# Routers of three layers: weights stand still, 512 turned tokens move, logits turned back

## The chip, the cores and the metric

One core of one Trainium2 chip. The metric is the device time of one execution of the kernel in microseconds (us). Engines: PE (TensorE, matrix multiplication), with PEld for its weight loads; DVE (VectorE); ACT (ScalarE); POOL (GpSimd); SP (SyncE, which here only issues transfers).

## What is computed

A stack of four layers on 32 x 256 = 8192 tokens of width 128, all in float32. Each layer is a mixing part and a part with experts, both added to the residual. Four times a router scores the tokens against the experts. For layers 0, 1 and 2, cut to what matters:

```
x = x + _L0_attn_ref(_layernorm(x), ...)
x = x + _L0_ffn_ref(_layernorm(x), ...)      # scores = softmax(h @ gate_w.T), 16 experts
x = x + _L1_attn_ref(_layernorm(x), ...)
x = x + _L1_ffn_ref(_layernorm(x), ...)      # logits = h @ gate_w + gate_b, 8 experts, top 2
x = x + _L2_attn_ref(_layernorm(x), ...)
x = x + _L2_ffn_ref(_layernorm(x), ...)      # logits = h @ router_W.T + router_b, 6 experts, top 2
```

Here `h` is the normalised x. Layer 3's router has 4 + 8 = 12 outputs and works on a normalisation with gain and offset.

## The kernel before

x stays on chip as 64 tiles of 128 tokens (tokens on the partitions). The kernel is a sequence of blocks; in most of them each engine runs its own loop over NU = 16 steps of UT = 4 tiles (U = 512 tokens), and the engines wait for each other by semaphores. A block ends when all engines have ended their loops; then the next begins.

`route` (line 849) is such a block. It is called for layer 0 as "d" (line 942, 16 outputs, no bias), for layer 1 as "m1" (line 1901, 8 outputs), for layer 2 as "m2" (line 2525, 6 outputs) and for layer 3 as "m3" (line 2752, 12 outputs, with `affine`). Its parts, for step n:

- DVE, `normed`: waits until PE has turned the tiles of step n - 3, then normalises four tiles (line 394, in `norm_tiles`) into one of S = 3 buffers nrm.
- PE, `turn`: transposes the four tiles (line 403, in `turn_tiles`) into a PSUM bank ps_t, so that the width is on the partitions and 512 tokens lie side by side.
- ACT, `keep`: copies the bank to hT (line 921), and for layers 1 and 2 first to h_all as well (line 920), which later loops use.
- PE, `project` (line 908): for each of the four tiles one matmul whose stationary operand is the tile of hT (128 x 128) and whose moving operand is the router's weights (16, 8 or 6 columns). The result has tokens on the partitions, in a bank ps_l. The first operand after the output in a `matmul` call is the stationary one.
- DVE, `keep`: waits for the logits and copies them to `logits` (line 892), or adds the bias on the way (line 894).

`staggered(eng, units, slots, *stages)` (line 107) sets the order on one engine: in step s it issues each stage in the order given, for unit s - lag. DVE runs (0, normed), (3, keep); PE runs (2, project), (0, turn); ACT runs (0, keep). An engine executes its instructions strictly in that order, and a wait holds up all that comes behind it. `sig.now(n, 1)` waits for unit n, `sig.ago(n, 1, S)` for unit n - S, `sig.last(n, 1)` for unit n - 1.
Of the kernel before, what the change touches and what calls it, by code (L numbers as in the profile page):

```python
# [12 lines left out]
ACT = mybir.ActivationFunctionType  # L13
# [4 lines left out]
ds = bass.ds  # L18

P = 128  # L20
# [3 lines left out]
UT = 4  # L24
U = UT * P
NU = NT // UT
# [80 lines left out]
def staggered(eng, units, slots, *stages):  # L107

    deep = max(lag for lag, _ in stages)
    rounds = (units - deep) // slots

    def step(i, s):
        for lag, work in stages:
            n = s - lag
            if i is not None:
                work(i * slots + n, n % slots, i + n // slots)
            elif 0 <= n < units:  # L120
                work(n, n % slots, n // slots)

    for s in range(deep):
        step(None, s)
    with eng.Fori(0, rounds) as i:  # L125
        for v in range(slots):
            step(i, deep + v)
    for s in range(deep + rounds * slots, units + deep):
        step(None, s)
# [43 lines left out]
def build(nc, x_in, pack_in, maskb_in, w0_in, w1_in, w3_in, out, ktab, ychan, q_stack, k_stack, ones_rows, v_ones,  # L173
          m_parts, xs1, xs3, ys):
    ctx = ExitStack()
    with ctx:
# [5 lines left out]
        def sig(name, per):  # L182
            return Signal(pool, name, per)

        def sb(name, shape, dt=F32, stack=ctx):
            return stack.enter_context(nc.sbuf_tensor(name, shape, dt))

        def bank(name, stack, n=1):
            return stack.enter_context(nc.psum_tensor(name, [P, n, 512], F32))
# [15 lines left out]
        ident = c("ident")  # L205
# [62 lines left out]
        routes = {}  # L268
        for t in ("d", "m1", "m2", "m3"):
            routes[t] = (Front(t, 1), sig(t + "_logits", 1), sig(t + "_logits_kept", 1), sig(t + "_affine", 2),  # L270
                         sig(t + "_src_kept", 1))
        g_n, g_p, g_mm, g_x = sig("g_normed", 4), sig("g_onehot", 4), sig("g_gathered", 4), sig("g_stored", 4)
        x_w, x_gu, x_ge, x_h, x_o, x_s = ([sig(f"x_weights{j}", 16) for j in range(2)], sig("x_gate_up", 8), sig("x_gelu", 8),
                                         sig("x_hidden", 8), sig("x_down", 4), sig("x_kept", 4))
# [123 lines left out]
        def turn_tiles(pe, done, ps, nrm, n, *waits):  # L398

            for w in waits:  # L400
                pe.wait_ge(*w)
            for t in range(n):
                ins = pe.transpose(ps[:, t * P:(t + 1) * P], nrm[:, t, :], ident)
            ins.then_inc(done.sem, 1)
# [133 lines left out]
        with ExitStack() as st_u:  # L538
            u_all = sb("u_all", [P, TPB, NB, INNER], stack=st_u)
            with ExitStack() as st:  # L540
                S = 4
                nrm = sb("a_nrm", [P, UT, P], stack=st)
                hT = [sb(f"a_hT{j}", [P, U], stack=st) for j in range(S)]
# [182 lines left out]
        with ExitStack() as st:  # L726
            S = 3
            nrm = sb("c_nrm", [P, UT, P], stack=st)
            hT = [sb(f"c_hT{j}", [P, U], stack=st) for j in range(S)]
# [119 lines left out]
        def route(tag, src, weights, bias, n_out, logits, h_all=None, affine=None, fetch=None):  # L849

            fr, lg, kept, aff, put = routes[tag]
            S = 3
            with ExitStack() as st:
                nrm = [sb(f"{tag}_nrm{j}", [P, UT, P], stack=st) for j in range(S)]
                hT = [sb(f"{tag}_hT{j}", [P, U], stack=st) for j in range(S)]
                ps_t = bank(f"{tag}_ps_t", st, S)
                ps_l = bank(f"{tag}_ps_l", st, S)  # L860
                with pool.loop_block(NU) as block:
                    if fetch is not None:
                        @block.sync
                        def _(sp):
                            w, w_in = fetch
                            for e in range(w.shape[1]):
                                n_filled[0] += 16
                                sp.dma_start(w[:, e, :], w_in[e]).then_inc(filled, 16)
                            sp.wait_ge(filled, n_filled[0])

                    @block.vector
                    def _(dve):
                        def normed(n, j, r):
                            free = fr.tps.ago(n, 1, S)
                            if affine is None:
                                norm_tiles(dve, fr.nrm, nrm[j], src, n * UT, UT, rstd, free)
                                return
                            dve.wait_ge(*put.ago(n, 1, S))
                            norm_tiles(dve, aff, nrm[j], src, n * UT, UT, rstd, free)
                            dve.wait_ge(*aff.now(n, 1))  # L880
                            dve.tensor_tensor(nrm[j][:, :, :], nrm[j][:, :, :],
                                              affine[0].unsqueeze(1).to_broadcast([P, UT, D]), ALU.mult).then_inc(aff.sem, 1)
                            dve.wait_ge(*aff.now(n, 2))
                            dve.tensor_tensor(nrm[j][:, :, :], nrm[j][:, :, :],
                                              affine[1].unsqueeze(1).to_broadcast([P, UT, D]), ALU.add
                                              ).then_inc(fr.nrm.sem, 1)

                        def keep(n, j, r):
                            dve.wait_ge(*lg.now(n, 1))
                            to, got = logits[:, ds(n * UT, UT), :], ps_l[:, j, 0:UT * n_out].rearrange("p (t e) -> p t e", t=UT)  # L890
                            if bias is None:
                                ins = dve.tensor_copy(to, got)
                            else:
                                ins = dve.tensor_tensor(to, got, bias.unsqueeze(1).to_broadcast([P, UT, n_out]), ALU.add)
                            ins.then_inc(kept.sem, 1)

                        staggered(dve, NU, S, (0, normed), (3, keep))

                    @block.tensor
                    def _(pe):  # L900
                        def turn(n, j, r):
                            turn_tiles(pe, fr.tps, ps_t[:, j, :], nrm[j], UT, fr.nrm.now(n, 1), fr.hT.ago(n, 1, S))

                        def project(n, j, r):
                            pe.wait_ge(*fr.hT.now(n, 1))
                            pe.wait_ge(*kept.ago(n, 1, S))
                            for t in range(UT):
                                ins = pe.matmul(ps_l[:, j, t * n_out:(t + 1) * n_out], hT[j][:, t * P:(t + 1) * P], weights,
                                                start=True, stop=True)
                            ins.then_inc(lg.sem, 1)  # L910

                        staggered(pe, NU, S, (2, project), (0, turn))

                    @block.scalar
                    def _(act):
                        def keep(n, j, r):
                            act.wait_ge(*fr.tps.now(n, 1))
                            act.wait_ge(*lg.ago(n, 1, S))
                            if h_all is not None:
                                act.activation(h_all[:, ds(n * U, U)], ps_t[:, j, :], ACT.Copy)  # L920
                            act.activation(hT[j][:, :], ps_t[:, j, :], ACT.Copy).then_inc(fr.hT.sem, 1)
                            if affine is not None:
                                act.activation(src[:, ds(n * UT, UT), :], nrm[j][:, :, :], ACT.Copy).then_inc(put.sem, 1)

                        staggered(act, NU, S, (0, keep))

        def softmax_rows(dve, lg, out_e, m, s, n):

# [10 lines left out]
        with ExitStack() as st_d:  # L939
# [72 lines left out]
            with ExitStack() as st_x:  # L1012
# [3 lines left out]
                with ExitStack() as st:  # L1016
                    S = 4
# [126 lines left out]
                with ExitStack() as st:  # L1144
                    S = 3
# [3 lines left out]
                    hT, hotT, eo, ge, hs = ([sb(f"f_{n}{j}", [P] + shape, stack=st) for j in range(S)] for n, shape in (  # L1149
                        ("hT", [SEQ]), ("hotT", [4, SEQ]), ("eo", [4, D]), ("ge", [2, SEQ]), ("hs", [2, SEQ])))  # L1150
# [123 lines left out]
        with ExitStack() as st:  # L1274
            VW = D + 4
            S = 6
            nrm, hT, egate, gate, qk, low, v1, am = (
                [sb(f"l_{n}{j}", [P] + shape, stack=st) for j in range(S)] for n, shape in (
                    ("nrm", [TPB, P]), ("hT", [SEQ]), ("egate", [SEQ]), ("gate", [SEQ]), ("qk", [2, SEQ]), ("low", [2, SEQ]),
                    ("v", [TPB, VW]), ("am", [P + SEQ])))  # L1280
# [614 lines left out]
        with ExitStack() as st1:  # L1895
# [3 lines left out]
            lg = sb("lg1", [P, NT, E1], stack=st1)  # L1899
            w = sb("w1", [P, E1, wide(F1)], stack=st1)  # L1900
            route("m1", x_res, c("gate1"), c("gate1b"), E1, lg, h_all, fetch=(w, w1_in))
            with ExitStack() as st:
                t1 = sb("m1_t", [P, NT], stack=st)
                with nc.Block() as block:
# [16 lines left out]
                    def _(act):  # L1921
# [3 lines left out]
                           normed=(h_all, x_res))  # L1925
# [595 lines left out]
        with ExitStack() as st2:  # L2521
            h_all = sb("h_all2", [P, NT * P], stack=st2)
            comb = sb("comb2", [P, NT, E2 + 1], stack=st2)
            lg = sb("lg2", [P, NT, E2], stack=st2)
# [28 lines left out]
            with ExitStack() as st:  # L2553
                S = 3
                hT = [sb(f"m_hT{j}", [P, U], stack=st) for j in range(S)]
# [79 lines left out]
        with ExitStack() as st:  # L2635
            S = 3
            nrm = sb("s_nrm", [P, UT, P], stack=st)
            hT = [sb(f"s_hT{j}", [P, 2, SEQ + 1], stack=st) for j in range(S)]
# [101 lines left out]
        with ExitStack() as st3:  # L2740
# [5 lines left out]
            with ExitStack() as st:  # L2746
# [4 lines left out]
                lg = sb("lg3", [P, NT, G3 + E3], stack=stl)  # L2751
# [40 lines left out]
            with ExitStack() as st:  # L2792
                S = 6
# [179 lines left out]
```

## Time and profile before

| | us |
|---|---|
| median of 3 runs | 3575.7 (3569.54 to 3576.92) |
| profiled execution, time | 3574.73 |
| its span | 3572.9 |
| PE busy in the span | 2609.7 (73%) |
| DVE busy | 2245.5 (63%) |
| ACT busy | 1580.3 (44%) |
| POOL busy | 634.1 (18%) |
| mean granted clock | 0.859 |

The span is the profiled part of one execution; the time has a little around it. PE's busy time is not PE at its peak, since passes overlap and also run at half clock. The granted clock of PE is 1.00 at 2.4 GHz and 0.50 at 1.2 GHz.

How the views are read. The page's slices cut the span into 40 equal parts. A window row gives the length of a stretch, the busy time of each engine with its number of instructions, the granted clock (PEclk), the share of the DMA engines that was busy, and what they moved. A timeline row gives start, duration (of a merged run: from first start to last end), engine, line, operation, tiles and form, count, and in brackets how long the engine had been idle before and what ended that. "128*128 128x16 f32" means 128 rows and 128 columns of weights, and a moving operand of 16 columns.

### The profile page before, as it was taken

To read this page: it belongs to the slowest core of one execution; us is meant where nothing else is said; L and a number is where in the kernel's file an instruction comes from. 1 tells how busy PE (TensorE), PEld (TensorE's weight loads), DVE (VectorE), ACT (ScalarE), POOL (GpSimd) and SP (SyncE) were. 2 spreads that over 40 slices of the span, in tenths; PEclk is the share of its full clock that TensorE was granted. 3 is DMA by queue.
4 is the path that set the end of the run, shared out by engine and by line. 5 is a ranking of instruction groups with operands and counts; after the bars stand their busy time and mean duration, and the time that the engine had idled before them with its cause. 6 is when DMAs were issued, how large, how long until landed. Compare 5 with 4: busy or idle time off the path is not lost. (4 is left out here: it accounts for less than half of the span.)

```text
span 3572.9 us, 72294 instructions
## 1 busy us (share of the span) xinstructions
PE 2609.7 (73%) x20194; PEld 1892.7 (53%) x20194; DVE 2245.5 (63%) x4945; ACT 1580.3 (44%) x3615; POOL 634.1 (18%) x873
## 2 busy tenths in 40 slices
PE   3546749999987576998339999966565999973280
PEld 1333444459877433998226777756333555552270
DVE  5924966248777422776846666645885777765267
ACT  2503613334364233775235666632253667751253
POOL 0000100000000265554301111100120111102553
PEclk7878959999998687999679999968797999985585
DMA  3096100100091011222494565400097555510123
GB/s 94 7 258 176 53 0 18 35 18 0 0 156 54 20 46 43 70 69 89 152 276 62 71 73 71 57 1 1 0 293 109 69 68 75 71 43 19 53 77 100
DMA packets 335935, 263.34 MB, mean 74 GB/s; under 512 B 23132, under 2 KB 317452, under 8 KB 335308
## 3 DMA queue, kind: packets, MB, share of 16 engines
q1 hardware_dynamic: 314200, 227.03, 31.5%
q0 software_dynamic: 12928, 26.70, 2.2%
q10 hardware_dynamic: 8704, 8.39, 0.8%
q8 instruction: 46, 0.75, 0.1%
q14 instruction: 57, 0.47, 0.0%
HBM read 145.60 MB, written 114.86 MB: 73 GB/s over the span
## 5 line engine op out<-in xcount | busy, mean ns | idle before, releaser
L2444 ACT ACTIVATE h_pt<-h_ps 128x384 f32<-128x384 f32 (+1 forms) x1024 | 543.6, 545 | 306.2 <-PE h_ps L2353 151.8
L2197 DVE TENSOR_REDUCE h_nm<-h_ps 128x4 f32<-128x1024 f32 (+1 forms) x448 | 539.7, 1220 | 163.4 <-PE h_ps L2324 64.0
L1606 POOL DMA_INDIRECT sorted_rows<-e_row,e_pos x192 | 185.1, 964 | 443.4 <-DVE e_row L1585 239.6
L2372 PE MATMUL h_ps_o<-h_pt,h_vp 128*32 128x256 f32 (+1 forms) x4096 | 246.8, 358 | 1.3 <-ACT h_pt L2444 1.3
L1796 POOL DMA_INDIRECT results<-e_y,e_ykey x208 | 211.0, 1015 | 193.6 <-DVE e_y L1785 176.7
L1843 ACT ACTIVATE e_hid<-e_ps_h,e_wt 128x128 f32<-128x128 f32 x688 | 204.3, 369 | 27.7 <-PE e_ps_h L1817 19.0
L2358 PE MATMUL h_ps<-h_sq,h_sk 128*128 128x256 bf16 x1024 | 193.6, 275 | 23.9 <-DMA h_sq<-m_parts 13.6
L1817 PE MATMUL e_ps_h<-e_hT,e_wt 128*128 128x128 f32 x1376 | 201.9, 288 | 6.3 <-issue 2.6
L1825 PE MATMUL e_ps_o<-e_wt,e_hid 128*128 128x128 f32 x1376 | 198.0, 283 | 11.2 <-ACT e_hid L1843 10.4
L1753 DVE TENSOR_SCALAR e_wt<-w 128x1156 f32 (+1 forms) x208 | 140.0, 673 | 98.5 <-DVE e_y L1785 69.8
L1817 PEld LDWEIGHTS e_ps_h<-e_hT,e_wt 128*128 128x128 f32 x1376 | 179.7, 201 | 14.2 <-issue 10.4
L1825 PEld LDWEIGHTS e_ps_o<-e_wt,e_hid 128*128 128x128 f32 x1376 | 178.2, 199 | 15.9 <-ACT e_hid L1843 13.5
L2295 PE MATMUL h_ps<-h_sk,h_sq 128*128 128x256 bf16 x1024 | 157.1, 277 | 39.7 <-DVE h_identb L2179 34.5
L2243 POOL TENSOR_TENSOR h_mpart<-h_nm,h_zero 128x32 bf16<-128x32 f32 x64 | 15.3, 240 | 892.5 <-DVE h_nm L2197 892.5
L2372 PEld LDWEIGHTS h_ps_o<-h_pt,h_vp 128*32 128x32 f32 x4096 | 106.8, 109 | 92.5 <-issue 36.7
L1810 PE MATMUL e_ps_t<-pack,e_xt 128*128 128x128 f32 x208 | 59.2, 286 | 124.9 <-DMA e_xt<-sorted_rows 124.3
L2350 PE MATMUL h_ps<-h_sq,h_sk 128*128 128x256 bf16 x512 | 140.6, 275 | 6.6 <-ACT h_pt L2444 2.8
L2353 PE MATMUL h_ps<-h_mskb 128*128 128x256 bf16 x512 | 139.6, 273 | 0.0
L1140 DVE TENSOR_TENSOR x_hid<-x_gelu,x_ps_u 128x512 f32<-128x512 f32 x64 | 43.4, 688 | 141.8 <-ACT x_gelu L1125 141.8
L2307 PE MATMUL h_ps<-h_sk,h_sq 128*128 128x256 bf16 x512 | 98.2, 274 | 45.7 <-DVE h_identb L2179 44.3
L2358 PEld LDWEIGHTS h_ps<-h_sq,h_sk 128*128 128x128 bf16 x1024 | 81.5, 98 | 93.1 <-ACT h_pt L2444 80.6
L2295 PEld LDWEIGHTS h_ps<-h_sk,h_sq 128*128 128x128 bf16 x1024 | 98.4, 99 | 58.7 <-DVE h_identb L2179 34.7
(435 smaller groups left out, 6170.8 us busy)
## 6 DMA issues: line engine op xcount, KB each, us to landing
h_sq<-q_stack SPq DMA_DIRECT2D x64, 384.0 KB
h_sk<-k_stack SPq DMA_DIRECT2D x64, 384.0 KB
sorted_rows<-pad SPq DMA_DIRECT2D x26, 520.0 KB, 11.7
e_xt<-sorted_rows SPq DMA_DIRECT2D x104, 130.0 KB, 2.2
e_got<-results SPq DMA_DIRECT2D x24, 512.0 KB, 5.9
q_stack<-p_parts SPq DMA_DIRECT2D x32, 384.0 KB, 3.1
k_stack<-p_parts SPq DMA_DIRECT2D x32, 384.0 KB, 3.8
v_ones<-p_v SPq DMA_DIRECT2D x32, 288.0 KB, 2.7
```

The costliest lines, as they stand in the source:

```text
L1606: gp.indirect_dma_start(xs[:, :], bass.IndirectOffsetOnAxis(ap=pos[:, n % choices, tile:tile + 1], axis=0), row[n % ROWS][:, :], None).the ...
L1753: dve.tensor_scalar(wt[j % 4][:, :], w[:, :, :].rearrange("p e w -> p (e w)")[:, ds(at, wc)], 1.0, None, ALU.mult).then_inc(e_w.sem, 1)
L1796: gp.indirect_dma_start(ys[:, :], bass.IndirectOffsetOnAxis(ap=key[m // 4][:, m % 4:m % 4 + 1], axis=0), y[m][:, :], None).then_inc(return ...
L1817: pe.matmul(ps_h[:, k, 0:P], wt[j % 4][:, f * P:(f + 1) * P], hT[j % 4][:, :], start=True, stop=True).then_inc(e_h.sem, 1)
L1825: ins = pe.matmul(o, hid_t[m][:, f, :], wt[m][:, f_dim + f * D:f_dim + (f + 1) * D], start=(f == 0), stop=(f == nf - 1))
L1843: act.activation(hid_t[j % 4][:, f, :], ps_h[:, (j * nf + f) % 4, 0:P], func, bias=wt[j % 4][:, o_b1 + f:o_b1 + f + 1]).then_inc(e_a.sem, 1)
L2197: dve.tensor_reduce(to, got, AX, ALU.max, negate=True).then_inc(s["mx"].sem, 1)
L2295: ins = pe.matmul(ps_1[:, h % 4, q * SEQ:(q + 1) * SEQ], sq[u][:, h, q * P:(q + 1) * P], sk[u][:, h, :], start=True, stop=True)
L2350: pe.matmul(o[:, 0:SEQ], sk[u][:, hd, 0:P], sq[u][:, hd, :], start=True, stop=False, skip_group_check=True)
L2358: ins = pe.matmul(o[:, t * SEQ:(t + 1) * SEQ], sk[u][:, hd, t * P:(t + 1) * P], sq[u][:, hd, :], start=True, stop=True)
L2372: ins = pe.matmul(ps_o[32 * j:32 * (j + 1), q0:], vp[u % 2][:, t, head(HG * g + j), :], pt[g % 2][:, j, t * SEQ:(t + 1) * SEQ - q0], start ...
L2444: act.activation(pt[g % 2][:, j, :], ps_2[:, h % 2, 0:SW], ACT.Exp, scale=scale).then_inc(s["ex"].sem, 1)
```

## The change

In `route`, where there is no `affine` (d, m1, m2), the logits are computed the other way round. The router's weights are the stationary operand and the 512 tokens of hT move, in one matmul; the logits come out with experts on the partitions (16, 8 or 6 of them) and 512 tokens side by side, in a bank ps_f of 3. ACT copies them to lT (`keep_flat`). PE turns them back with four matmuls whose stationary operand is a piece of lT (16, 8 or 6 rows, 128 columns) and whose moving operand is the corner of the unit matrix (16, 8 or 6 columns), into a single bank ps_l. DVE's `keep` comes a step later (lag 4) and reads from that bank. PE runs (3, turn_back), (2, project_flat), (0, turn); ACT runs (0, keep), (2, keep_flat). Layer 3's router is unchanged.

```diff
--- before.py
+++ after.py
@@ -268,7 +268,7 @@
         routes = {}
         for t in ("d", "m1", "m2", "m3"):
             routes[t] = (Front(t, 1), sig(t + "_logits", 1), sig(t + "_logits_kept", 1), sig(t + "_affine", 2),
-                         sig(t + "_src_kept", 1))
+                         sig(t + "_src_kept", 1), sig(t + "_logits_flat", 1), sig(t + "_flat_kept", 1))
         g_n, g_p, g_mm, g_x = sig("g_normed", 4), sig("g_onehot", 4), sig("g_gathered", 4), sig("g_stored", 4)
         x_w, x_gu, x_ge, x_h, x_o, x_s = ([sig(f"x_weights{j}", 16) for j in range(2)], sig("x_gate_up", 8), sig("x_gelu", 8),
                                          sig("x_hidden", 8), sig("x_down", 4), sig("x_kept", 4))
@@ -851,13 +851,17 @@
 
 
 
-            fr, lg, kept, aff, put = routes[tag]
+            fr, lg, kept, aff, put, flat, flat_kept = routes[tag]
+            by_expert = affine is None
             S = 3
             with ExitStack() as st:
                 nrm = [sb(f"{tag}_nrm{j}", [P, UT, P], stack=st) for j in range(S)]
                 hT = [sb(f"{tag}_hT{j}", [P, U], stack=st) for j in range(S)]
                 ps_t = bank(f"{tag}_ps_t", st, S)
-                ps_l = bank(f"{tag}_ps_l", st, S)
+                if by_expert:
+                    lT = [sb(f"{tag}_lT{j}", [n_out, U], stack=st) for j in range(S)]
+                    ps_f = bank(f"{tag}_ps_f", st, S)
+                ps_l = bank(f"{tag}_ps_l", st, 1 if by_expert else S)
                 with pool.loop_block(NU) as block:
                     if fetch is not None:
                         @block.sync
@@ -887,19 +891,33 @@
 
                         def keep(n, j, r):
                             dve.wait_ge(*lg.now(n, 1))
-                            to, got = logits[:, ds(n * UT, UT), :], ps_l[:, j, 0:UT * n_out].rearrange("p (t e) -> p t e", t=UT)
+                            to = logits[:, ds(n * UT, UT), :]
+                            got = ps_l[:, 0 if by_expert else j, 0:UT * n_out].rearrange("p (t e) -> p t e", t=UT)
                             if bias is None:
                                 ins = dve.tensor_copy(to, got)
                             else:
                                 ins = dve.tensor_tensor(to, got, bias.unsqueeze(1).to_broadcast([P, UT, n_out]), ALU.add)
                             ins.then_inc(kept.sem, 1)
 
-                        staggered(dve, NU, S, (0, normed), (3, keep))
+                        staggered(dve, NU, S, (0, normed), (4 if by_expert else 3, keep))
 
                     @block.tensor
                     def _(pe):
                         def turn(n, j, r):
                             turn_tiles(pe, fr.tps, ps_t[:, j, :], nrm[j], UT, fr.nrm.now(n, 1), fr.hT.ago(n, 1, S))
+
+                        def project_flat(n, j, r):
+                            pe.wait_ge(*fr.hT.now(n, 1))
+                            pe.wait_ge(*flat_kept.ago(n, 1, S))
+                            pe.matmul(ps_f[0:n_out, j, :], weights, hT[j][:, :], start=True, stop=True).then_inc(flat.sem, 1)
+
+                        def turn_back(n, j, r):
+                            pe.wait_ge(*flat_kept.now(n, 1))
+                            pe.wait_ge(*kept.last(n, 1))
+                            for t in range(UT):
+                                ins = pe.matmul(ps_l[:, 0, t * n_out:(t + 1) * n_out], lT[j][:, t * P:(t + 1) * P],
+                                                ident[0:n_out, 0:n_out], start=True, stop=True)
+                            ins.then_inc(lg.sem, 1)
 
                         def project(n, j, r):
                             pe.wait_ge(*fr.hT.now(n, 1))
@@ -909,20 +927,31 @@
                                                 start=True, stop=True)
                             ins.then_inc(lg.sem, 1)
 
-                        staggered(pe, NU, S, (2, project), (0, turn))
+                        if by_expert:
+                            staggered(pe, NU, S, (3, turn_back), (2, project_flat), (0, turn))
+                        else:
+                            staggered(pe, NU, S, (2, project), (0, turn))
 
                     @block.scalar
                     def _(act):
+                        def keep_flat(n, j, r):
+                            act.wait_ge(*flat.now(n, 1))
+                            act.wait_ge(*lg.ago(n, 1, S))
+                            act.activation(lT[j][:, :], ps_f[0:n_out, j, :], ACT.Copy).then_inc(flat_kept.sem, 1)
+
                         def keep(n, j, r):
                             act.wait_ge(*fr.tps.now(n, 1))
-                            act.wait_ge(*lg.ago(n, 1, S))
+                            act.wait_ge(*(flat if by_expert else lg).ago(n, 1, S))
                             if h_all is not None:
                                 act.activation(h_all[:, ds(n * U, U)], ps_t[:, j, :], ACT.Copy)
                             act.activation(hT[j][:, :], ps_t[:, j, :], ACT.Copy).then_inc(fr.hT.sem, 1)
                             if affine is not None:
                                 act.activation(src[:, ds(n * UT, UT), :], nrm[j][:, :, :], ACT.Copy).then_inc(put.sem, 1)
 
-                        staggered(act, NU, S, (0, keep))
+                        if by_expert:
+                            staggered(act, NU, S, (0, keep), (2, keep_flat))
+                        else:
+                            staggered(act, NU, S, (0, keep))
 
         def softmax_rows(dve, lg, out_e, m, s, n):
```

## Rows read from the trace of the kernel before

**Rows 1.** The page: the span, and the clock in 40 slices (tenths).

```profile
span 3572.9 us, 72294 instructions
...
PEclk7878959999998687999679999968797999985585
```

**Rows 2.** Windows, three stretches: length, busy us by engine, clock, DMA, GB/s.

```profile
454.00:495.50 41.50, 39.89 (x192) 39.26 (x192) 21.29 (x80) 9.55 (x16) 0.00 (x0) 0.50 0.00 1
1145.00:1188.00 43.00, 40.06 (x192) 39.26 (x192) 21.39 (x81) 17.76 (x33) 0.00 (x0) 0.50 0.29 111
2353.00:2395.00 42.00, 40.06 (x192) 39.27 (x192) 20.20 (x80) 17.76 (x33) 0.00 (x0) 0.50 0.00 0
```

**Rows 3.** Waits in 454 to 495.5 us: waiter, releaser, us in total, times, longest.

```profile
ACT d_hT L921 <- PE d_ps_t L403: 31.1, 16, 4.6
```

**Rows 4.** Timeline, layer 0's router: start us, us, engine, line, operation, tiles, form.

```profile
453.94 4.19 DVE L394 TENSOR_SCALAR d_nrm<-x_res,mean,rstd 128x128 f32<-128x128 f32 x16 [0.55 <-PEq L343]
...
457.07 1.88 PE L908 MATMUL d_ps_l<-pack,d_hT 128*128 128x16 f32 x8
...
461.25 1.09 PE L403 MATMUL d_ps_t<-pack,d_nrm 128*128 128x128 f32 x4
...
461.92 1.83 PEld L908 LDWEIGHTS d_ps_l<-pack,d_hT 128*128 128x128 f32 x8
...
462.46 0.60 ACT L921 ACTIVATE d_hT<-d_ps_t 128x512 f32<-128x512 f32 x1 [1.86 <-PE d_ps_t L403]
...
464.38 1.83 PEld L908 LDWEIGHTS d_ps_l<-pack,d_hT 128*128 128x128 f32 x8
...
495.05 0.23 DVE L892 COPY d_score<-d_ps_l 128x64 f32<-128x64 f32 x1 [1.48 <-PE d_ps_l L908]
```

**Rows 5.** Lines 908, 403, 2706: count, ns min/median/max, starts, form.

```profile
L908 PE MATMUL d_ps_l<-pack,d_hT x128: 234/374/388, 457.1 to 494.6; 128*128 128x16 f32 x128
...
L403 PE MATMUL d_ps_t<-pack,d_nrm x64: 421/421/476, 455.1 to 491.4; 128*128 128x128 f32 x64
...
L2706 PE MATMUL s_ps_h<-s_mix,pack x32: 592/697/1222, 2494.2 to 2573.6; 128*128 128x512 f32 x32
```

**Rows 6.** Timeline, layer 1's router, start and end.

```profile
1148.40 0.59 ACT L921 ACTIVATE m_hT<-m_ps_t 128x512 f32<-128x512 f32 x1
...
1149.12 1.78 PEld L908 LDWEIGHTS m_ps_l<-pack,m_hT 128*128 128x128 f32 x8 [0.79 <-issue]
...
1152.16 0.60 ACT L920 ACTIVATE h_all<-m_ps_t 128x512 f32 x1 [2.12 <-PE m_ps_t L403]
1152.65 0.59 ACT L921 ACTIVATE m_hT<-m_ps_t 128x512 f32<-128x512 f32 x1
...
1187.09 0.19 DVE L894 TENSOR_TENSOR lg<-m_ps_l,pack 128x32 f32<-128x32 f32 x1 [1.52 <-PE m_ps_l L908]
```

**Rows 7.** Timeline, layer 0's first loop, clock at half.

```profile
68.02 3.78 PE L598 MATMUL a_ps_u<-a_hT,pack 128*128 128x512 f32 x4 [0.92 <-ACT a_hT L620]
...
71.59 1.06 PE L403 MATMUL a_ps_t<-pack,a_nrm 128*128 128x128 f32 x4
```

**Rows 8.** Timeline, weights with 32 active rows, clock at half.

```profile
1735.01 0.84 PE L2502 MATMUL w_ps<-pack,w_turned 32*128 32x128 f32 x3
```

**Rows 9.** Timeline, PE in two stretches at full clock.

```profile
816.15 1.06 PE L1239 MATMUL f_ps_o<-f_eo,f_hotT 128*128 128x128 f32 x8
...
765.50 1.02 PE L1104 MATMUL x_ps_u<-xg,x_w 128*128 x2
766.36 1.02 PE L1102 MATMUL x_ps_g<-xg,x_w 128*128 x2
```

**Rows 10.** Groups of ACT by form: the copy of 113 partitions.

```profile
L2629 ACT ACTIVATE m_hwT<-m_ps_t 113x512 f32<-113x512 f32 x16 | 9.6, 597 | 31.2 <-PE m_ps_t L2605 31.2
```

**Rows 11.** Windows over layer 0's first loop and layer 3's scan loop.

```profile
62.00:162.00 100.00, 62.63 (x240) 34.40 (x240) 88.01 (x183) 55.25 (x83) 0.00 (x0) 0.86 0.00 0
2486.00:2580.00 94.00, 56.93 (x224) 37.59 (x224) 81.75 (x212) 19.94 (x32) 20.38 (x16) 0.76 0.00 0
```

## The prediction

> **What bounds the kernel now.** The time is a long row of loops that run one after another, so each loop is judged alone and only three are touched: the routers of layers 0, 1 and 2. I read the windows over them first [rows 2]. PE is busy 39.9 of 41.5 us, 40.1 of 43.0 and 40.1 of 42.0; DVE has about half, ACT 9.6 to 17.8. The waits say the same: ACT sat 31.1 us before its copies, and it was always PE's transposes that ended it [rows 3]. The clock column is what to look at next: 0.50 in all three stretches although PE is never idle, that is 1.2 GHz; the page's slices show it too [rows 1, 2].
>
> The timeline gives the step [rows 4]: the weight loads of one projection start at 461.92, of the next at 464.38, so 2.46 us for 4 tiles. In it lie 8 passes of L908 (4 float32 matmuls show as 8 records) and 4 of L403. A pass that streams only 16 columns costs as much as one with 128: after an idle spell 8 passes lasted 1.88 us, the last of them 0.37 [rows 4, 5], so they follow each other by 1.51 / 7 = 0.215 us. The weight load of 128 columns sets that.
>
> **The change part by part.** m3 keeps its old path (it has `affine`). In the other three, a step of 512 tokens changes as follows, priced at the clock of 0.50 first.
>
> *Removed:* 8 passes with 128 tokens as weights, 1.7 us.
>
> *Added, flat projection:* one float32 matmul, weights of 16, 8 or 6 columns, 512 columns moving, so two passes. In layer 0's first loop at half clock four such passes start at 68.02 and the next operation at 71.59 [rows 7]: 0.85 each with the start-up taken off, so 1.71 us. Its narrow weight load is hidden behind the stream, as the 128-column ones there are.
>
> *Added, turning back:* 4 matmuls, so 8 passes, whose weights are lT: 16, 8 or 6 rows, but again 128 columns. Do fewer rows load faster? The nearest row is w_ps with 32 active rows: three passes in 0.84 us, of which the last about 0.42, so 0.21 apart [rows 8], the price of 128 rows. I take 1.72 us until the next pass can start. From below I bound it by 0.11 a pass, the full-clock pitch [rows 9]: (1.06 - 0.27) / 7.
>
> So the cost that should go comes back in full, and 1.71 us of streaming come on top: PE's own work rises from 2.46 to 1.70 + 1.71 + 0.85 = 4.26 us a step. *The DVE copy* moves one step later and is as large as before; it and the four normalisations (16 took 4.19 us [rows 4], 1.05 for four) stay covered. The single ps_l bank makes turn_back(n) wait for DVE's copy of n-1, whose input is ready a whole PE step earlier: nothing, under that cover; about 0.5 us a step without it.
>
> *Added, ACT's copy,* and this is the second large term. Follow the order written in the program. PE in step s: turn_back(s-3), flat(s-2), turn(s). ACT in step s: keep(s), which waits for turn(s), the last thing PE does, and only then keep_flat(s-2). The next PE step begins with turn_back(s-2), which waits for that very copy. Everything else on PE is queued behind it. So PE sleeps from the end of its transposes until ACT has done both copies, in each step; no lag is left over, though the stages look three deep. The terms:
> - transposes' end (461.25 + 1.09) to ACT's start (462.46): 0.12 us [rows 4];
> - the hT copy: the next ACT instruction starts 0.49 later (1152.16 to 1152.65) [rows 6]; layers 1 and 2 have h_all too, 0.49 more;
> - the flat copy: 0.60, taken from 512 elements on 113 partitions, 597 ns, which is also the time of 128 [rows 10, 4]; from below 0 if few partitions were free of charge;
> - ACT's end to PE: 1148.40 + 0.59 to 1149.12, 0.13 [rows 6].
>
> Step at half clock, layer 0: turn back 1.72, flat 1.71, four transposes 3 x 0.213 + 0.42 = 1.06, then 0.12 + 0.49 + 0.60 + 0.13: 5.83 us. Layers 1 and 2: 6.32.
>
> *The sum.* Layer 0: flat(0) can start where the projection does, at 457.07; the first turn back follows after 5.83 - 1.72 = 4.11, at 461.2. Then 13 full steps (3 to 15), 75.8: 537.0. Two steps of the tail without transposes: 1.72 + 0.85, the last pass 1.22 [rows 5], 0.12 + 0.60 + 0.13 = 4.64 each: 546.3. The last turn back 1.88: 548.2, where the last copy starts at 495.05 now [rows 4]: +53 us. Layers 1 and 2: 1149.12 + 4.11 + 0.49 = 1153.7; 13 x 6.32 = 82.2; tail 9.3; last 1.9: 1247.1 instead of 1187.09 [rows 6], +60 each. In all +173 us. Nothing runs beside the routers that this could cover (layer 1's weight transfers end long before), and no later loop starts from anything else. The profiled execution took 3574.7 us, span 3572.9, and lies 1.0 under the median of 3575.7; on it the sum gives 3748, on the median 3749.
>
> **The clock.** The half clock is shown for these stretches as they are; the change streams 1024 columns more per step, in a step over twice as long, with PE asleep for 1.3 to 1.8 us of it. Two loops with passes of 512 columns are the nearest rows: layer 0's first loop had a mean of 0.86, layer 3's scan 0.76 [rows 11]. Both stream more per microsecond than the new router would (the first has four 512-column passes a step to the router's two; the scan adds, by its code, eight passes of 128 columns where the router has eight of 16). I take 0.50 and keep the rest as a rival. The Trainium skill ("TensorE: Matmul & The Clock Gate", Part 1) says that "the default state is throttled, and activity releases the throttle". Read simply, a PE that is always busy should run at 2.4 GHz; this trace disagrees, at 0.50 over 40 us of busy PE [rows 2]. By that rule the new router, too, would be at full clock: rival 2.
>
> **The rivals.**
> 1. *The clock alternates*, as in rows 11. With a mean near 0.75, half the time passes at either level: between forecast and rival 2, about 3698.
> 2. *The clock is full.* Turn back 0.90, flat 0.86 (765.50 to 766.36 holds two passes of 512), transposes 0.60 [rows 9], ACT as before: 3.70 us, 4.19 in layers 1 and 2. That is 2.13 less per full step, 27.7 for 13, and some 6 in fill and tail: +73 in all, 3648.
> 3. *The copy is hidden, clock at half*: if ACT reached the flat copy while PE still worked. Then PE alone, 4.26 - 2.46 = 1.80 x 48 = +87: 3662. The order of the two stages on ACT speaks against it.
> 4. *The other side: faster.* One mechanism: the 512-column passes release the clock and ACT's copies lie beside PE's work. A step is then 0.87 + 0.86 + 0.44 = 2.17 us (ACT needs 1.6 at most), 0.29 less than now, times 48: -14, 3562. It decides once both hold; with the wait alone left, 3.70 is already above 2.46.
> 5. *The turn back is cheaper* because few rows are loaded: at 0.11 a pass 0.86 less a step, 41 in all, 3708.
>
> **How the numbers follow.** Forecast 0.68; rival 1 0.16; rival 2 0.04; rival 3 0.03; rival 4 0.02; rival 5 0.04; something unforeseen 0.03. The forecast's own spread: the free flat copy would take off 0.6 x 48 = 29, and the reckoning of the added wait values by the queues, which nothing covers while PE sleeps, could add up to 0.5 us a step (the lag seen without cover is 0.12 to 0.13 now), 24 in all. So 3720 to 3773 for it, and down to 3690 for rivals 1 and 5. A difference of 0.2%, 7 us, is about what can be told from no change; only rival 4 and the least likely of the rest come near it: faster 0.02, same 0.01, slower 0.97.
>
> **What would show it.** Right: PE idle once a step before turn_back, released by ACT's flat copy, 1.3 us in layer 0 and 1.8 in 1 and 2; steps of 5.8 and 6.3 us; turn-back passes 0.21 apart; clock 0.50; router stretches of 94 to 102 us. m3 and all other loops unchanged. Wrong: turn_back released by something else or by nothing (rival 3), a clock above 0.50 (1, 2), turn-back passes clearly under 0.2 apart at half clock (5).

## The result and the profile after

The changed kernel takes 3726.8 us (median of 4 runs, 3721.8 to 3730.7) against 3572.8 for the kernel before, 1.043 times as long, 95% interval 1.0409 to 1.045. The forecast was 3749, range 3690 to 3775.

The page of after, its span (compare [rows 1]):

```profile
span 3728.1 us, 72918 instructions
```

The windows over the three routers, with the columns of [rows 2]:

```profile
450.00:542.00 92.00, 72.06 (x224) 39.80 (x224) 21.35 (x80) 17.34 (x33) 0.00 (x0) 0.54 0.00 0
1190.00:1293.00 103.00, 74.14 (x224) 40.70 (x224) 20.99 (x82) 25.26 (x49) 0.00 (x0) 0.52 0.12 46
2457.00:2556.00 99.00, 70.93 (x224) 39.05 (x224) 20.41 (x80) 24.87 (x49) 0.00 (x0) 0.55 0.00 0
```

They have grown from 41.5, 43 and 42 us to 92, 103 and 99; DVE's work is about the same (21.4, 21.0, 20.4 us), PE is idle for 20 to 29 us in each, and the clock, 0.50 before, is 0.54, 0.52 and 0.55. From the first normalisation to the last copy of logits I measure 41.3 + 41.9 + 41.8 = 125.0 us before and 91.6 + 101.7 + 98.5 = 291.8 after: 167 us. The two profiled spans differ by only 155. The other 12 lie outside the routers: 4 before the first, some 5 between the third and layer 3's; layer 3's own router took 47.2 and 46.9. A second profile of the same kernel (below) shows 277.2 us for the three, where I had expected the same 292; most of the difference, 11.6 us, is in layer 0. So one profile's stretches can differ from another's by some 15 us.

One step in layer 0's router, from its transposes to the next step's turn back (answers to [rows 4]):

```profile
461.11 1.12 PE L403 MATMUL d_ps_t<-pack,d_nrm 128*128 128x128 f32 x4
462.26 0.60 ACT L947 ACTIVATE d_hT<-d_ps_t 128x512 f32<-128x512 f32 x1 [4.91 <-PE d_ps_t L403]
462.76 0.57 ACT L940 ACTIVATE d_lT<-d_ps_f 16x512 f32<-16x512 f32 x1
...
463.38 1.88 PE L918 MATMUL d_ps_l<-pack,d_lT 16*128 16x16 f32 x8 [1.15 <-ACT d_lT L940]
...
465.19 1.89 PE L912 MATMUL d_ps_f<-d_hT,pack 128*16 128x512 f32 x2
...
467.01 1.12 PE L403 MATMUL d_ps_t<-pack,d_nrm 128*128 128x128 f32 x4
...
469.28 1.77 PEld L918 LDWEIGHTS d_ps_l<-pack,d_lT 16*128 16x128 f32 x8 [1.55 <-ACT d_lT L940]
```

Read it as a chain. Transposes (461.11, end 462.23), ACT's copy to hT (462.26), ACT's flat copy (462.76, 16 partitions, 0.57 us), and in the moment when that ends (463.33) PE begins to turn back. It had been idle for 1.15 us. Then the flat projection (465.19), the transposes (467.01), ACT again (468.17). From 463.38 to 469.28 is 5.90 us, against 2.46 before. In the list of groups, what PE waited for before the turn back (the last figures; m_ps_l is layers 1 and 2 together):

```profile
L918 PE MATMUL m_ps_l<-pack,m_lT 8*128 8x8 f32 (+1 forms) x256 | 56.5, 344 | 52.0 <-ACT m_lT L940 52.0
...
L918 PE MATMUL d_ps_l<-pack,d_lT 16*128 16x16 f32 x128 | 28.5, 357 | 18.1 <-ACT d_lT L940 18.1
```

18.1 + 52.0 = 70 us of waiting, all released by ACT's flat copy. In layers 1 and 2 a step's wait is mostly 1.73 us.

### The profile page after: what moved, and what is told of

It reads as the page before. It is cut to its first block and busy times, and to the rows that moved or that the text cites. A ratio compares the mean times of both kernels' runs of the same rounds, so it can differ in the third digit from the quotient of the medians.

```text
span 3728.1 us, 72918 instructions
## 1 busy us (share of the span) xinstructions
PE 2695.8 (72%) x20290; PEld 1886.1 (51%) x20290; DVE 2245.6 (60%) x4945; ACT 1600.8 (43%) x3663; POOL 632.6 (17%) x873
## 5 line engine op out<-in xcount | busy, mean ns | idle before, releaser
L2226 DVE TENSOR_REDUCE h_nm<-h_ps 128x4 f32<-128x1024 f32 (+1 forms) x448 | 539.9, 1220 | 159.3 <-PE h_ps L2353 61.2
L1846 PEld LDWEIGHTS e_ps_h<-e_hT,e_wt 128*128 128x128 f32 x1376 | 175.4, 197 | 26.5 <-issue 19.6
```

The lines of the kernel that those rows point to most:

```text
L1846: pe.matmul(ps_h[:, k, 0:P], wt[j % 4][:, f * P:(f + 1) * P], hT[j % 4][:, :], start=True, stop=True).then_inc(e_h.sem, 1)
L2226: dve.tensor_reduce(to, got, AX, ALU.max, negate=True).then_inc(s["mx"].sem, 1)
```

## The experiments

Each kernel was timed beside the kernel before on the same chip. e1 to e4 ran on one chip, e5 to e7 and the change again on a second, e8 on a third; the kernel before took 3526, 3579 and 3569 us on them, so only ratios and the stretches are compared between them. "Stretch" is the time from a router's first normalisation to its last copy of logits, of the one profiled execution; "clock" is PE's mean granted clock in it.

| kernel | stretches of layers 0, 1, 2, us | sum | clock | time over before (95%) |
|---|---|---|---|---|
| before | 41.3, 41.9, 41.8 | 125.0 | 0.50, 0.50, 0.50 | 1 |
| the change | 91.6, 101.7, 98.5 | 291.8 | 0.54, 0.52, 0.55 | 1.043 (1.0409 to 1.045) |
| the change again | 80.0, 98.7, 98.5 | 277.2 | 0.67, 0.55, 0.55 | 1.0424 (1.0403 to 1.0445) |
| e8, before and the wait | 58.7, 67.3, 67.5 | 193.5 | 0.50, 0.50, 0.50 | 1.0186 (1.0169 to 1.0203) |
| e4, before and a stream | 51.4, 45.1, 42.6 | 139.1 | 0.77, 0.88, 0.94 | 1.0052 (1.0021 to 1.0082) |
| e7, change and a stream | 66.3, 75.7, 73.8 | 215.8 | 0.94, 0.91, 0.94 | 1.0241 (1.0224 to 1.0258) |
| e1, flat copy first | 56.4, 61.2, 49.4 | 167.0 | 0.77, 0.70, 0.91 | 1.0081 (1.0065 to 1.0098) |
| e2, later turn back | 45.5, 46.0, 44.4 | 135.9 | 0.91, 0.91, 0.95 | 1.003 (1.0019 to 1.0042) |
| e3, one pass | 56.8, 77.0, 76.5 | 210.3 | 0.95, 0.73, 0.73 | 1.0261 (1.0241 to 1.028) |
| e6, e2 and e3 | 36.5, 37.7, 37.7 | 111.9 | 0.91, 0.92, 0.91 | 0.9954 (0.994 to 0.9969) |
| e5, packed | 25.3, 26.5, 25.9 | 77.7 | 0.87, 0.89, 0.89 | 0.9866 (0.985 to 0.9883) |

**e1: the wait, by ACT's order.**

```diff
-                            staggered(act, NU, S, (0, keep), (2, keep_flat))
+                            staggered(act, NU, S, (2, keep_flat), (0, keep))
```

> The change, with ACT's two stages in the other order: first the flat copy of n-2, then the copies of n. Theory W (the wait comes from the order on ACT): the flat copy runs while PE transposes, so PE's idle time before the turn back falls from 1.15 us (layer 0) and 1.7 us (layers 1, 2) to about 0.3 us, since the last pass of the flat projection ends late. Step 4.55 us at half clock instead of 5.9 and 6.35: 15 x 1.35 + 30 x 1.8 = 74 us less than 3727, so 3653; still less if the denser PE gets full clock (step 2.75 us), down to 3575. Rival B (PE waits for the single bank of logits, or its own work sets the step): no change, 3717 to 3737.

Measured 1.0081. Of the change's 1.043 four fifths are gone by exchanging two stages, without a change in any operation. Windows, and one step of layer 0:

```profile
455.00:511.50 56.50, 52.20 (x224) 29.35 (x224) 21.32 (x80) 18.70 (x32) 0.00 (x0) 0.77 0.00 0
1157.90:1219.10 61.20, 57.17 (x224) 32.26 (x224) 20.55 (x80) 26.69 (x48) 0.00 (x0) 0.70 0.20 78
2353.40:2402.80 49.40, 44.59 (x224) 25.35 (x224) 20.40 (x80) 26.68 (x48) 0.00 (x0) 0.91 0.00 0
```

```profile
480.24 0.66 PE L403 MATMUL d_ps_t<-pack,d_nrm 128*128 128x128 f32 x4
480.34 0.59 ACT L940 ACTIVATE d_lT<-d_ps_f 16x512 f32<-16x512 f32 x1 [1.59 <-PE d_ps_f L912]
...
480.98 1.06 PE L918 MATMUL d_ps_l<-pack,d_lT 16*128 16x16 f32 x8
```

The flat copy (480.34) now lies beside the transposes, and PE turns back at 480.98, 0.05 after the copy ends. The profiled execution was the slowest of the four, 12 to 17 us above the others, so its stretches show a larger loss (42 us against the kernel before) than the ratio does (29 us). The clock rose too, to between 0.70 and 0.91, so the run lies between my two figures (1.022 at half clock by 3653, 1.000 by 3575); it says that the wait mattered, not how much of the gain was wait and how much clock. Rival B is out: the single bank is still there, and the time fell.

**e2: the wait, by a later turn back.**

```diff
-                            staggered(pe, NU, S, (3, turn_back), (2, project_flat), (0, turn))
+                            staggered(pe, NU, S, (4, turn_back), (2, project_flat), (0, turn))
```

and DVE's copy at lag 5.

> The change, with the turn back one step later (lag 4, DVE's copy lag 5), ACT's order as in the change. Theory W: each flat copy has a whole step of slack, PE is never idle. PE alone at half clock: 1.70 + 1.71 + 0.85 = 4.26 us a step, 45 x about 1.9 = 86 us less, 3641. Theory C (512-column streams release the clock once PE does not sleep): step near 2.2 us, some 90 us less again, 3550 to 3590, faster than the kernel before. Rival B (the bank of logits): no change, 3717 to 3737.

Measured 1.003, with the clock at 0.91 to 0.95:

```profile
451.40:497.00 45.60, 43.65 (x224) 25.15 (x224) 20.95 (x80) 17.25 (x32) 0.00 (x0) 0.91 0.00 1
1148.30:1194.20 45.90, 43.69 (x224) 25.37 (x224) 20.42 (x80) 24.76 (x48) 0.00 (x0) 0.91 0.27 103
2330.70:2375.10 44.40, 42.17 (x224) 24.22 (x224) 20.28 (x80) 24.76 (x48) 0.00 (x0) 0.95 0.00 1
```

```profile
472.06 1.06 PE L918 MATMUL d_ps_l<-pack,d_lT 16*128 16x16 f32 x8
...
473.05 1.03 PE L912 MATMUL d_ps_f<-d_hT,pack 128*16 128x512 f32 x2
...
474.02 0.66 PE L403 MATMUL d_ps_t<-pack,d_nrm 128*128 128x128 f32 x4
...
474.60 1.06 PE L918 MATMUL d_ps_l<-pack,d_lT 16*128 16x16 f32 x8
```

Before the turn back no wait for ACT is left, and the clock is nearly full, as theory C said. But a step is 2.54 us and not 2.2: from one group to the next PE needs 0.99, 0.97 and 0.58 us where the bare passes gave 0.87, 0.86 and 0.44, about 0.12 for each hand-over. At nearly full clock and with nothing waiting, the new form is a little slower than the old form at half clock.

**e3: what the turn back costs.**

```diff
-                                ins = pe.matmul(ps_l[:, 0, t * n_out:(t + 1) * n_out], lT[j][:, t * P:(t + 1) * P],
-                                                ident[0:n_out, 0:n_out], start=True, stop=True)
+                                ins = pe.transpose(ps_l[:, 0, t * P:(t + 1) * P], lT[j][:, t * P:(t + 1) * P], ident)
```

> The change, with the turn back as four real transposes of 128 rows, one pass each, instead of four float32 matmuls of two passes; lT has 128 rows, of which those beyond the experts are zeroed once. Theory L (the turn back costs its number of passes, about 0.215 us each at half clock): 4 passes less, 0.86 us a step, 41 us less than 3727: 3686. Rival: rows or columns moved count, or the turn back is covered: 3720 or more, since each pass moves 128 columns instead of 16, 8 or 6.

Measured 1.0261, about 60 us under the change where 41 were expected:

```profile
457.40:514.20 56.80, 37.21 (x160) 15.95 (x160) 21.07 (x80) 17.24 (x32) 0.00 (x0) 0.95 0.00 0
1164.90:1241.90 77.00, 49.29 (x160) 19.30 (x160) 20.85 (x80) 24.79 (x48) 0.00 (x0) 0.73 0.15 59
2377.60:2454.10 76.50, 48.86 (x160) 19.72 (x160) 20.40 (x80) 24.78 (x48) 0.00 (x0) 0.73 0.00 0
```

The direction is theory L's; the total is not, because the clock did not hold still: 0.95 in layer 0 and 0.73 in the others. The price of the passes has to be read from steps at half clock (line 926 is the turn back, 920 the flat projection here):

```profile
1221.35 1.12 PE L926 MATMUL m_ps_l<-pack,m_lT 128*128 128x128 f32 x4 [1.73 <-ACT m_lT L948]
1222.39 1.87 PE L920 MATMUL m_ps_f<-m_hT,pack 128*8 128x512 f32 x2
```

The four passes need 1.04 us until the next group starts; the change's eight needed 1.81 (2527.41 to 2529.22 below). That is 0.77 us less a step where theory L said 0.86, 37 us of the expected 41; the rest of the gain goes with the higher clock. The rival is out: each pass moves 128 columns instead of 8 or 6, and the group is shorter. One more thing is to be seen. PE still waits for ACT as long as in the change (1.73 us in this step), and in layer 0 it is busy for 37.2 of 56.8 us against 72.1 of 92.0, yet the clock is higher. So the higher clock of e1 and e2 can't be put down to the missing wait alone; what decides it, these runs don't show.

**e8: the wait alone.**

```diff
-                            pe.wait_ge(*fr.hT.now(n, 1))
+                            ahead = 0 if affine is not None or (isinstance(n, int) and n == NU - 1) else 1
+                            pe.wait_ge(*fr.hT.now(n, 1 + ahead))
```

in `project` of the kernel before.

> The kernel before, with one wait moved in the three routers and no work added: the projection of n waits for ACT's copies of n+1, which wait for the transposes that PE issued just before. Theory W at half clock: PE idle for 0.12 + 0.60 + 0.13 = 0.85 us a step in layer 0 and 1.33 in layers 1 and 2, clock still 0.50, in all 15 x 0.85 + 30 x 1.33 = 53 us less what the first pass now hides (0.2 a step, 9): 44 to 53 us more, ratio 1.012 to 1.015. Rival (the queues absorb such a wait): below 1.004.

Measured 1.0186, more than the 1.012 to 1.015 expected. The windows, and a step of layer 0 (the old projection is line 909 here):

```profile
453.70:512.40 58.70, 45.20 (x192) 38.80 (x192) 21.34 (x80) 9.56 (x16) 0.00 (x0) 0.50 0.00 0
1163.90:1231.20 67.30, 45.21 (x192) 38.83 (x192) 20.99 (x80) 17.33 (x32) 0.00 (x0) 0.50 0.18 71
2397.10:2464.60 67.50, 45.17 (x192) 38.81 (x192) 20.45 (x80) 17.32 (x32) 0.00 (x0) 0.50 0.00 0
```

```profile
472.45 1.78 PEld L909 LDWEIGHTS d_ps_l<-pack,d_hT 128*128 128x128 f32 x8 [1.24 <-issue]
472.46 1.89 PE L909 MATMUL d_ps_l<-pack,d_hT 128*128 128x16 f32 x8 [0.84 <-ACT d_hT L922]
...
476.04 1.78 PEld L909 LDWEIGHTS d_ps_l<-pack,d_hT 128*128 128x128 f32 x8 [1.17 <-ACT d_hT L922]
476.05 1.89 PE L909 MATMUL d_ps_l<-pack,d_hT 128*128 128x16 f32 x8 [0.77 <-ACT d_hT L922]
```

The clock stayed at 0.50 in all three, so this is the price of such a wait by itself: 193.5 - 125.0 = 68.5 us. PE's visible idle time is 0.84 and 0.77, near the 0.85 expected, yet the step grew from 2.46 to 3.59, by 1.1. I had taken 0.2 off because PE might hide something; the sign was wrong. The rows of the weight loads show what else was lost: they sat idle for 1.24 and 1.17 us. Before, the first weight load of a group ran under the last transpose (at 461.92 [rows 4]), and the projection began 0.20 us before the transposes' end (462.34):

```profile
462.14 1.73 PE L908 MATMUL d_ps_l<-pack,d_hT 128*128 128x16 f32 x8
```

Behind a wait that overlap is gone, and the eight passes last 1.89 instead of 1.73 us: 0.2 + 0.16 us on top of the 0.77.

**e4: a stream added to the kernel before.** It leaves the result as it is.

```diff
+                            if affine is None:
+                                pe.matmul(ps_x[0:n_out, 0, :], weights, hT[j][:, :], start=True, stop=True)
```

> The kernel before, with the flat projection of the change added in each step of the three routers, into a bank that nobody reads. Nothing waits for it. If the clock stays at half: two passes of 512 columns, 1.71 us in each of 48 steps, 82 us more: 3655. Theory C (such streams release the clock): step 2.2 to 2.5 us with all passes at full clock, 3555 to 3580: more work in no more time.

Measured 1.0052: the flat projection added to all 48 steps, 82 us of passes at half clock, costs 14 us in the stretches and 18 us by the ratio.

```profile
454.10:505.50 51.40, 49.94 (x224) 28.36 (x224) 21.34 (x80) 9.56 (x16) 0.00 (x0) 0.77 0.00 0
1153.80:1198.90 45.10, 43.30 (x224) 24.54 (x224) 20.99 (x80) 17.33 (x32) 0.00 (x0) 0.88 0.27 106
2336.70:2379.30 42.60, 40.83 (x224) 23.23 (x224) 20.50 (x80) 17.32 (x32) 0.00 (x0) 0.94 0.00 0
```

The clock is the reason. The added pass pair at four places of layer 0:

```profile
471.04 1.89 PE L909 MATMUL d_ps_x<-d_hT,pack 128*16 128x512 f32 x2
...
475.62 1.89 PE L909 MATMUL d_ps_x<-d_hT,pack 128*16 128x512 f32 x2
...
484.13 1.03 PE L909 MATMUL d_ps_x<-d_hT,pack 128*16 128x512 f32 x2
...
486.57 1.03 PE L909 MATMUL d_ps_x<-d_hT,pack 128*16 128x512 f32 x2
```

1.89 us each at the beginning, 4.6 apart; 1.03 each later, 2.44 apart. That is the step of the kernel before (2.46) with 70% more work in it. PE was hardly idle in either kernel (busy 49.9 of 51.4 us here); what differs is that two passes of 512 columns were added to eight that move 16, 8 or 6 and four transposes that move 128. Where the clock rose late, in layer 0, the stretch is 10 us longer; where it rose early, in layer 2, 1 us. The ten timed runs spread from 3528.6 to 3567.3, wider than any other kernel's: three took 3564 to 3567 us with a mean granted clock of 0.871 to 0.875 over the whole kernel, the other seven 3529 to 3541 with 0.881 to 0.884. That fits a clock that rises later in some executions, but only one of the quick seven was profiled, so where it was lost stays open.

**e7: a stream in the gap of the changed kernel.**

```diff
+                            if by_expert:
+                                pe.matmul(ps_x[0:n_out, 0, :], weights, pack[:, 0:U], start=True, stop=True)
```

after the transposes of each step, into a bank that nobody reads.

> The change, with one more float32 matmul of 512 columns after the transposes of each step, from a constant part of the inputs into a bank that nobody reads: PE works in the time in which it slept; the wait for ACT's flat copy stays as it is. Theory C (the clock is a term of its own, released by streamed columns): full clock, steps of 3.7 and 4.2 us instead of 5.9 and 6.35, the three router stretches together some 95 us shorter than with the change, 1.02 of the kernel before. Rival W (the wait is the whole difference between the change and e2): no gain, 1.04 to 1.05, as the added passes at half clock are as long as the gap.

Measured 1.0241 where the change itself had 1.0424 in the same call. One more matmul in each step makes the kernel 63 us faster.

```profile
453.10:519.40 66.30, 60.22 (x256) 26.95 (x256) 21.52 (x80) 17.27 (x32) 0.00 (x0) 0.94 0.00 0
2414.00:2487.80 73.80, 59.76 (x256) 26.63 (x256) 20.46 (x80) 24.93 (x48) 0.00 (x0) 0.94 0.00 0
```

```profile
479.94 0.66 PE L403 MATMUL d_ps_t<-pack,d_nrm 128*128 128x128 f32 x4
...
480.52 1.03 PE L911 MATMUL d_ps_x<-pack 128*16 128x512 f32 x2
...
481.75 1.06 PE L922 MATMUL d_ps_l<-pack,d_lT 16*128 16x16 f32 x8 [0.19 <-ACT d_lT L944]
```

ACT's chain is as long as it was: from the transposes' end (480.60) to the turn back it is 1.15 us, as in the change, only that PE now works in most of it. The clock is 0.91 to 0.94. So the half clock is a term of its own in the change's loss, worth 60 to 75 us (by the ratios 0.0183 x 3579 = 65; by the stretches 277.2 - 215.8 = 61 or 291.8 - 215.8 = 76). I had expected 95: steps of layer 0 take 3.8 to 3.9 us instead of 3.7, and the change, from which the gain is counted, already had some steps at full clock.

**e6: both mends.** e2 and e3 together.

> e2 and e3 together: turn back one step later, as four one-pass transposes. PE's work at full clock 0.44 + 0.86 + 0.44 and 0.2 between them, 1.9 to 2.0 us a step against 2.46 in the kernel before: 22 to 27 us less, ratio 0.992 to 0.994. If the clock falls back to half: 3.4 us a step, 45 us more, 1.013.

Measured 0.9954, 0.0046 x 3579 = 16 us less than the kernel before; the stretches are 13 us shorter in sum. The expected 22 to 27 was too much: steps are about 2.0 us, the upper end of my figure (in layer 0 the turn backs start at 472.35 and 474.33), and fill and tail are longer by a step.

**e5: packed, a version that beats both.** The weights, padded with zeros to 32 columns, meet the four tiles of a step one by one, each with an output of its own 32 partitions. Then one copy of 128 x 128 and one transpose turn all four back. ACT's order is that of e1. The parts of the edit that matter:

```diff
-                            pe.matmul(ps_f[0:n_out, j, :], weights, hT[j][:, :], start=True, stop=True).then_inc(flat.sem, 1)
+                            for t in range(UT):
+                                ins = pe.matmul(ps_f[32 * t:32 * (t + 1), j, 0:P], w32[:, :], hT[j][:, t * P:(t + 1) * P],
+                                                start=True, stop=True, skip_group_check=True)
+                            ins.then_inc(flat.sem, 1)
...
-                            for t in range(UT):
-                                ins = pe.matmul(ps_l[:, 0, t * n_out:(t + 1) * n_out], lT[j][:, t * P:(t + 1) * P],
-                                                ident[0:n_out, 0:n_out], start=True, stop=True)
-                            ins.then_inc(lg.sem, 1)
+                            pe.transpose(ps_l[:, 0, 0:P], lT[j][:, :], ident).then_inc(lg.sem, 1)
...
-                            staggered(act, NU, S, (0, keep), (2, keep_flat))
+                            staggered(act, NU, S, (2, keep_flat), (0, keep))
```

> Flat logits of the four tiles of a step on four groups of 32 output partitions (weights padded to 32 columns, 128 tokens moving each), so that one copy of 128 x 128 and one transpose turn them all back; the flat copy comes first on ACT. PE: two passes of 128 columns if the four groups run at once, else eight, one transpose pass, four transposes: 1.5 to 1.7 us a step at half clock with groups at once, 2.8 without. With groups at once DVE (1.4 to 1.6) is nearly the bound: 0.85 us a step less than before, 41 in all, ratio 0.988 to 0.991. Without: 1.005.

Measured 0.9866, 48 us less than the kernel before; the stretches say 125.0 - 77.7 = 47.

```profile
457.80:483.20 25.40, 21.58 (x208) 12.89 (x208) 20.12 (x80) 13.84 (x32) 0.00 (x0) 0.87 0.00 1
1134.20:1160.70 26.50, 21.97 (x208) 12.48 (x208) 19.75 (x80) 20.17 (x48) 0.00 (x0) 0.89 0.46 179
2326.00:2352.00 26.00, 21.35 (x208) 12.49 (x208) 19.41 (x80) 19.59 (x48) 0.00 (x0) 0.89 0.00 0
```

```profile
470.15 0.66 PE L403 MATMUL d_ps_t<-pack,d_nrm 128*128 128x128 f32 x4
...
471.03 0.42 PE L922 MATMUL d_ps_f<-d_hT,d_w 128*32 128x128 f32 x8
```

Eight passes of 128 columns together last 0.42 us (471.03): the four groups of output partitions run at once; one after another, at the 0.11 a pass of [rows 9], they would take 0.87. No single engine sets the time: PE is busy for 21 to 22 of some 26 us and DVE for 19 to 20, and before three of layer 0's turn backs PE waits 0.4 to 0.5 us for DVE's copy out of the single bank. The clock is 0.87 to 0.89 here, which I had not counted on, and the ratio is a little below the expected 0.988 to 0.991.

## Why the prediction was right, and where it was off

**The wait for ACT: right, and shown.** The chain of rows stands in the trace as forecast: 1.15 us of PE idle in layer 0 (forecast 1.3) and 1.73 in layers 1 and 2 (forecast 1.8), 70 us in all. e1 and e2, which only move stages, take most of the loss away, part of it by the clock; e8 puts such a wait alone into the kernel before and costs 68 us there. By my terms it would be 44 to 53: they lacked the lost overlap behind the wait, about 0.3 us a step (1.13 - 0.84).

**The turn back: right for its passes.** 8 passes of 16 rows last 1.88 us (463.38), exactly the 1.88 of 128 rows behind an idle spell [rows 4]: rows don't count. What the change removed and what it added in that place are nearly the same; e3 at half clock confirms that passes are what is paid.

**The flat projection: right.** 1.82 us from its start to the next group, forecast 1.71. The 0.1 more fits the weight load of the transposes, which did not start ahead: in the next step it begins together with its matmul, at 472.91.

**The steps.** 5.90 us for 5.83. For layers 1 and 2, 6.46 (2527.41 to 2533.87 below), for 6.32. All at half clock. That they agree so well is in part luck: PE's three groups took 1.81 + 1.82 + 1.12 = 4.75 us where I had 4.49, since each group lacked its head start, and the wait took 1.15 where I had 1.34. The two errors nearly cancel. What I allowed for the queues, up to 0.5 us a step, is in no row: PE starts 0.05 us after ACT's copy ends, and at most one step in three is 0.16 us longer.

**The clock: the forecast's first choice held only in part.** I took 0.50 throughout and gave 0.16 to an alternating clock. It does alternate, but seldom. In layer 2's router:

```profile
2527.41 1.87 PE L918 MATMUL m_ps_l<-pack,m_lT 6*128 6x6 f32 x8 [1.73 <-ACT m_lT L940]
...
2529.22 1.88 PE L912 MATMUL m_ps_f<-m_hT,pack 128*6 128x512 f32 x2
...
2533.87 1.05 PE L918 MATMUL m_ps_l<-pack,m_lT 6*128 6x6 f32 x8 [1.73 <-ACT m_lT L940]
...
2534.85 1.03 PE L912 MATMUL m_ps_f<-m_hT,pack 128*6 128x512 f32 x2
```

The step that begins at 2527.41 has its passes at half clock (turn back 1.87, flat 1.88), the next at full (1.05, 1.03), and it ends after 4.7 us: about 1.8 less. That, and the tail (4.38 us a step for my 4.64), offset what the steps were longer: the stretches grew by 50.3, 59.8 and 56.6 us for 53, 60 and 60 forecast. Six of the 48 turn backs ran at full clock in this profile, 14 in the second one, which has layer 0 at a clock of 0.67 and 11.6 us shorter. That is rival 1 in a small part, mixed into the forecast.

The forecast of 3749 lies 22 above the median. 3 of these are the kernel before, whose median is 3572.8 with one more run and not 3575.7. By the first profile 6 are the stretches (173 forecast, 167 found) and the other 13 lie nearly all outside the routers, in work that the change doesn't touch. By the second profile it is the other way round: the stretches grew by 152 us, 21 less than forecast, and nothing is left outside (the medians there differ by 148). So how the 22 us divide differs from execution to execution, and the cause of the part outside is not known.

**The rivals.** Rival 3 (copy hidden, half clock) was priced at +87 and was not met by itself: in e1 and e2, where the copy is hidden, the clock rose as well. Rival 4 named both conditions and promised 14 us; e2 meets both, but for a clock of 0.91 to 0.95, and is 0.3% slower than before, since hand-overs between groups cost 0.12 us each, which the sum of bare passes left out. Rival 5 is refuted by the row of 16 rows. Rival 2's case, full clock with the wait in place, is what e7 made: +91 us in the stretches (215.8 - 125.0) where rival 2 said +73, with the hand-overs missing there too.

The Trainium skill's sentence ("TensorE: Matmul & The Clock Gate", Part 1) that activity releases the throttle was set against 40 us of busy PE at 0.50. By its plain reading the kernel before should have been at full clock, and it was not; with streams added, the clock was 0.77 to 0.94 (e4) and 0.91 to 0.94 (e7), which agrees with it. What counts as activity no run here shows.

## What to carry to other kernels

A software pipeline can look three stages deep and still have no slack. It happens when, on a second engine, the short stage that the next step needs first stands behind the stage that waits for this step's last work. Write down for each engine what its first instruction of a step waits for, and whether that comes from the last one of the step before. Count passes before turning a small result: here eight passes with 16 rows of weights and 16 columns moving took as long as with 128 rows. Better, collect several small results on different output partitions and turn them back together. And when PE is busy but at half clock, read the granted clock beside the busy share: the same work may be had for less, and a run with added passes shows whether it is so.

## What the runs showed of the hardware that I had not expected

- More work in less time: one more float32 matmul of 512 columns a step made the changed kernel 0.0183 of 3579 us faster (e7), and cost the kernel before 0.5% instead of the 2.3% that the passes take at half clock (e4).
- Four float32 matmuls with 32 output partitions each and 128 columns moving, 8 passes, last 0.42 us together (e5).
- A wait costs more than the idle time of matmuls shows: 0.77 to 0.84 us of it went with 1.1 us of step (e8), since the group behind it no longer overlaps with the one ahead (0.2 us) and lasts longer itself (1.89 for 1.73).
- ACT's copy of 512 columns costs 0.57 to 0.59 us on 6, 8 or 16 partitions, about as much as on 128 (0.60) (the change).
